# First attention of a four-layer kernel: the output projection of unit u-2 moves behind the sums of unit u, into the free bank of their pair and in four 32-column tiles; the row maxima are turned in 64x64 tiles

## What is computed

```python
# B=2, T=1024, D=128, 16 heads, head size 8 for q and k, 64 for v
cp   = leaky_relu(x @ Wc.T + bc)
q, k, v = cp[..., :128], cp[..., 128:256], cp[..., 256:]
attn = softmax(q @ k.T / sqrt(8))            # per head, 1024 x 1024
out  = attn @ v                              # 16 heads x 64 columns = 1024
s    = leaky_relu(out @ Wo.T + bo) + x
```

## Time and profile before

| | |
|---|---|
| time, median of 3 runs | 1037.55 us |
| the runs | 1035.93, 1037.55, 1039.93 us |
| profiled execution: span from the first to the last instruction | 1034.0 us |
| profiled execution: own time | not listed apart from the span; the median is 3.5 us above the span |
| TensorE busy (matmuls) | 926.5 us, 90% |
| VectorE, GpSimd, ScalarE busy | 773.7, 633.5, 547.7 us |
| mean granted TensorE clock | 0.955 |
| attention, sums of unit 0 to sums of unit 28 | 185.1 to 590.7 us |
| attention, its last three units and end | 590.7 to 653.5 us |

### The profile page before, as it was taken

The page is one execution under the profiler, slowest core; times in us unless marked ns, Lnnn a source line. Parts: engine busy times, 40 slices in busy tenths (PEclk is TensorE's granted clock), DMA queues, the critical chain, the costliest instruction groups (busy, mean ns, idle before and its releaser), DMA issues.

```text
span 1034.0 us, 20151 instructions
## 1 busy us (share of the span) xinstructions
PE 926.5 (90%) x7298; PEld 476.8 (46%) x7298; DVE 773.7 (75%) x1300; ACT 547.7 (53%) x927; POOL 633.5 (61%) x555
## 2 busy tenths in 40 slices
PE   5799997999999999999989997799966766799997
PEld 3346554233333333333323334788955322368785
DVE  5864777888888888887888726774599999995513
ACT  1474445666666666666657784342454032257363
POOL 5570415788778667886877882033567878862412
PEclk9899998999999999999999998899999797799999
DMA  9353424111020101011101123467830200234562
GB/s 318 136 182 116 137 79 130 45 48 47 17 57 28 57 23 49 30 54 54 39 21 45 39 74 112 159 203 211 276 106 10 72 22 19 96 94 144 146 192 67
DMA packets 92273, 96.99 MB, mean 94 GB/s; under 512 B 23184, under 2 KB 68624, under 8 KB 91920
## 3 DMA queue, kind: packets, MB, share of 16 engines
q1 hardware_dynamic: 87056, 85.21, 27.0%
q0 software_dynamic: 5120, 10.50, 3.4%
HBM read 70.43 MB, written 24.77 MB: 92 GB/s over the span
## 4 chain that ended last, share of the span: by engine, by line
PE 74%; DVE 12%; POOL 5%; issue 4%; DMA 2%; ACT 1%; SPq 0%; DVEq 0%; ACTq 0%; POOLq 0%
PE ps L255 71%; PE ps L258 3%; POOL ar L261 3%; DVE small L274 3%; DVE ar L261 2%; DVE ar L274 1%; POOL psum_sb L261 1%; DVE osb L274 1%; DVE acc_sb L261 1%; DMA psum_sb<-in_L_bv 1%; DVE ps L261 1%; DVE psum_sb L261 1%; POOL acc_sb L320 1%; POOL gT L320 0%; SPq L301 0%
## 5 line engine op out<-in xcount | busy, mean ns | idle before, releaser
L255 PE MATMUL ps<-ar 64*64 64x512 bf16 (+4 forms) x5312 | 541.1, 448 | 36.6 <-DVE ar L261 12.3
L255 PEld LDWEIGHTS ps<-ar 64*64 64x64 bf16 (+2 forms) x5312 | 268.5, 137 | 288.8 <-issue 102.3
L298 ACT ACTIVATE ar<-ps 128x1024 f32<-128x1024 f32 (+2 forms) x336 | 303.9, 908 | 156.7 <-PE ps L255 150.9
L274 DVE TENSOR_REDUCE small<-ps 128x2 f32<-128x1024 f32 (+2 forms) x276 | 307.1, 1139 | 46.3 <-PE ps L255 44.7
L261 POOL TENSOR_TENSOR psum_sb<-psum_sb,ar 128x1024 f32<-128x1024 f32 x91 | 214.8, 2360 | 48.8 <-DVE on_sb L261 38.6
L261 POOL TENSOR_TENSOR ar<-ar 128x512 f32<-128x512 f32 (+1 forms) x80 | 106.4, 1333 | 36.1 <-DVE ar L274 18.3
L320 POOL DMA_INDIRECT gT<-ysort,rt x48 | 46.0, 958 | 99.7 <-issue 98.5
L261 DVE TENSOR_TENSOR ar<-ps,ar 128x256 f32<-128x256 f32 (+4 forms) x56 | 56.5, 1012 | 52.0 <-PE ps L255 43.3
L261 POOL TENSOR_TENSOR psum_sb<-ar 128x1024 f32<-128x1024 f32 x32 | 75.8, 2368 | 27.9 <-ACT ar L298 25.1
L295 ACT COPY ar<-ps 128x256 f32<-128x256 f32 (+1 forms) x84 | 30.8, 383 | 88.1 <-PE ps L255 53.0
L255 PE MATMUL ps<-wA,xnT 128*128 128x512 f32 (+3 forms) x192 | 66.6, 461 | 4.7 <-DVE ar L261 1.6
(11 more groups left out here) (159 smaller groups left out, 1050.0 us busy)
## 6 DMA issues: line engine op xcount, KB each, us to landing
ar<-in_L_up SPq DMA_DIRECT2D x48, 384.0 KB, 4.0
ar<-in_L_b SPq DMA_DIRECT2D x32, 322.0 KB, 3.6
rec_sb<-lscr SPq DMA_DIRECT2D x64, 128.0 KB
scr<-ar SPq DMA_DIRECT2D x48, 128.0 KB, 2.0
ar<-xsort SPq DMA_DIRECT2D x40, 128.0 KB, 2.4
ysort<-ar SPq DMA_DIRECT2D x40, 128.0 KB, 3.8
ar<-scr SPq DMA_DIRECT2D x32, 112.0 KB
xsort<-xs SPq DMA_DIRECT2D x12, 256.0 KB, 6.8
```

Source lines behind the costliest of these rows:

```text
L255: return self.e.matmul(o, l, r, start=start, stop=stop) if self.e else Nothing()
L274: return self.e.tensor_reduce(o, a, AX.X, op, negate=True) if negate else self.e.tensor_reduce(o, a, AX.X, op)
L298: return self.e.activation(o, a, fn, **kw) if self.e else Nothing()
```

## The change

The projection of unit u leaves k = 12 for k = 17, that is from step 8u+20 to step 8u+25, the step of the sums of unit u+2; there it follows the sums directly, writes into the second bank of their pair instead of a pair of its own, and is cut into four matmuls of 32 output columns. VectorE's `acc_sb` piece goes from k = 12 to k = 18. Units 30 and 31 keep k = 12. The turned maxima (but for the first ones) become two 64x64 transposes into the two banks of a pair, with one copy over both. The waits name both banks of a pair. In `SIDE_B` all pieces behind about step 125 stand 6 steps later, and none later than 256.

```diff
+    def proj_step(u):
+
+        return 17 if u < 30 else 12
...
-            for b in banks:
+            for b in banks if len(banks) > 1 else (banks[0], banks[0] + 1):
                 pe.wait_ge(*vacant(b))
...
-            pe.tr(pb[0:48, 0:128], nsp[:, 48 * k:48 * k + 48], identb).then_inc(*filled(b, ("rowsT", B)))
+            pe.wait_ge(*vacant(b + 1))
+            for n in range(2):
+                r = slice(64 * n, 64 * n + 64)
+                ins = pe.tr(ps[:, b + n, :].bitcast(BF16)[0:48, 0:64], nsp[r, 48 * k:48 * k + 48], identb[r, r])
+            ins.then_inc(*filled(b, ("rowsT", B)))
...
             if k == 1:
                 b = take(ring[0])
                 pe.wait_ge(*vacant(b))
+                pe.wait_ge(*vacant(b + 1))
+                beside_sums[u] = b + 1
...
-            if k == 12:
+            if k == proj_step(u):
                 pi = 2 * (g % 4) + pr
-                b = take(ring[0])
+                b = beside_sums[u + 2] if u < 30 else take(ring[0])
                 pe.wait_ge(*vacant(b))
                 pe.wait_ge(*at("scaled", u))
...
-                pe.mm(ps[:, b, :], wA[:, 1280 + 128 * pi:1408 + 128 * pi],
-                      on_sb[:, 512 * (u % 2):512 * (u % 2) + 512]).then_inc(*filled(b, ("proj", u)))
+                for r in range(0, 128, 32):
+                    ins = pe.mm(ps[r:r + 32, b, :], wA[:, 1280 + 128 * pi + r:1312 + 128 * pi + r],
+                                on_sb[:, 512 * (u % 2):512 * (u % 2) + 512])
+                ins.then_inc(*filled(b, ("proj", u)))
...
+            unit_tail(x // 8 - 3, x % 8 + 16)
...
                 s, b0 = g % 3, take(ring[0])
                 pe.wait_ge(*vacant(b0))
+                pe.wait_ge(*vacant(b0 + 1))
...
-            if k == 12:
+            if k == (18 if u < 30 else 12):
                 pi = 2 * (g % 4) + pr
                 dst = acc_sb[:, c0:c0 + CW]
                 dve.wait_ge(*at("proj", u))
...
-        "207 route.2 211 route.2 213 route.2 route.2 route.2 ln.1.0 220 route.2 ln.1.0 221 route.2 222 route.2 223 "
+        "213 route.2 217 route.2 219 route.2 route.2 route.2 ln.1.0 226 route.2 ln.1.0 227 route.2 228 route.2 229 "
```

More of the change, by code:

```diff
@@ L681, in tensor_program @@
         ring = [(4, 5, 6, 7)]
+        beside_sums = {}
         def ln(layer, c):
@@ L748, in max_rows @@
             pe.wait_ge(*at("rows_split", B))
-            pe.tr(pb[0:48, 0:128], nsp[:, 48 * k:48 * k + 48], identb).then_inc(*filled(b, ("rowsT", B)))
+            if B == 0:
+                pe.tr(pb[0:48, 0:128], nsp[:, 0:48], identb).then_inc(*filled(b, ("rowsT", B)))
+                return
+            pe.wait_ge(*vacant(b + 1))
[3 more added lines that the diff above has]
+            ins.then_inc(*filled(b, ("rowsT", B)))
         def max0():
@@ L1803, in max_rows @@
                 act.wait_ge(*at("rows1_in", B - 2))
-            pb = ps[:, bank["rowsT", B], :].bitcast(BF16)
-            act.acp(mT[:, 128 * k:128 * k + 128], pb[0:48, 0:128]).then_inc(*emptied(("rowsT", B), ("rows", B)))
+            b, dst = bank["rowsT", B], mT[:, 128 * k:128 * k + 128]
+            if B == 0:
+                ins = act.acp(dst, ps[:, b, :].bitcast(BF16)[0:48, 0:128])
+            else:
+                ins = act.acp(v3(dst, 64), ps[0:48, b:b + 2, :].bitcast(BF16)[:, :, 0:64])
+            ins.then_inc(*emptied(("rowsT", B), ("rows", B)))
         def max0():
```

## The result

The changed kernel takes 1094.2 us (median of 4 runs, 1092.33 to 1095.38) against 1037.12 for the kernel before (4 runs): a ratio of 1.057 with a 95% interval of 1.0541 to 1.0598, slower by 57 us. The forecast was 1073 with a range to 1088; the direction was right, the size 21 us short. The span of the profiled execution is 1090.5 us, 56.5 more than before.

A forecast was written before the change was run, and what follows sets the result against it. TensorE was taken as the bound (98% busy). Waits less savings +33.4, two exceptions -0.9, turned maxima -2.7, first and last units -2.7, end +8.8 sum to +35.9 on 1034.0; with 3.5 for the median, 1073 us, range 1058 to 1088.

The forecast's parts named there:

- The wait: In 24 units TensorE's scores of step 3 wait for VectorE's `acc_sb` to free their bank: 1.84 us each.
- the two exceptions: Two units where side work takes the pair first: wait covered, only 0.45 us of savings left each, -0.9 together.
- The savings: On TensorE per unit: 0.29 us from the projection behind the sums, 0.16 from the scores of step 3 and their maxima.
- Turned maxima: In every second unit their extra 0.64 us goes, but a new wait of 0.43 comes: -2.7 us in all.
- The end: Behind the sums of unit 31: the late last scatter delays SyncE's row loads and all behind, +8.8 us, bounds 0 and 9.8.
- The side work that moves by six steps: Side pieces shifted in the table meet other moments of VectorE: costed at nothing, bound 4 us either way.
- one scatter stands between GpSimd's last additions: In the last units, with unit 29's reciprocal no longer behind an `acc_sb`: together -0.7 us.
- The clock rival: TensorE's clock falls in half of the 24 new waits, 1.65 us lost each: +20, 1093 us; chance 0.10.

The follow-up runs named there:

- e1_acc17: The changed kernel with VectorE adding the projection one step earlier (k = 17), ahead of the reduction: 1137.13 us, ratio 1.0215 to the kernel before.
- e4_tiles_only: The kernel before with only the projection cut into four 32-column matmuls at its old place (k = 12): ratio 0.9987.
- e9_one_scatter: The kernel before with one GpSimd scatter moved from behind step 246 to behind step 252: 1128.73 against 1119.42 us, ratio 1.0073.
- e2_side_only: The kernel before with only the new side table, shifted by six steps: 1135.49 against 1114.5 us, ratio 1.0182.
- e19_pool_late: The kernel before with only GpSimd's side entries from step 216 on moved six steps later: 1131.46 against 1114.41 us, ratio 1.0163.
- e16_after_early: The changed kernel, but in the side table only entries from 127 to 164 move by six: 1156.31 us against 1119.92 for the kernel before, ratio 1.0324.
- before_again: The kernel before, unchanged, traced again on one of the four chips of the experiments: sums of unit 0 to 31 in 444.2 us.
- e7_pool_free: The kernel before without GpSimd's wait for `scaled` at k = 2: 1160.13 against 1119.92 us, ratio 1.0346.

## Why the prediction was wrong

**The wait: right, and 0.09 too small.** Four rows gave 2.91 - 1.07 = 1.84, and by the same count the trace has 3.01 - 1.07, some 1.93; the difference is the last row, 0.83 where 0.74 was taken. In 24 units that is 2 us. 24 of 26 units have it, and the two exceptions are units 19 and 25. But they didn't give back 0.45: unit 19 takes 16.95 us instead of 13.88. TensorE waits there 1.06 us for VectorE's side piece `xs`, which stands ahead of the reduction, and 1.05 for GpSimd at its end.

**The savings: right.** Without the wait a unit is 13.29 (`e1_acc17`), 0.45 under before, just 0.29 + 0.16. The parts come out too. In `e1_acc17` the scores of step 3 start 4.03 us behind the sums, before 3.17: the projection takes 0.86 there, against 1.16 at its old place. And the maxima follow these scores after 0.22 instead of 0.39. `e4_tiles_only` shows that the 0.29 is not the tiles' alone (0.06) but needs the place behind the sums, as the prediction had it. The savings are there beside the wait too: 13.74 + 1.93 - 0.46 = 15.21.

**Turned maxima: right in sum, by some luck.** 0.43 taken, 15.66 - 15.21 = 0.45. The prediction had the transposes below 0.1 and hidden in a wait of 0.43; in the trace they take 0.19, and the maxima two groups behind start 0.2 later than elsewhere:

```profile
345.67 0.41 PE L255 MATMUL ps<-ar 64*64 64x512 bf16 x4
...
346.12 0.41 PE L255 MATMUL ps<-ar 64*64 64x512 bf16 x4
```

The reduction that has to free their pair ends at 346.07.

**The end: right.** +8.8 forecast, +10.2 in the profile, +8.2 in the times of `e9_one_scatter`.

**The step that failed** is "The side work that moves by six steps meets other moments of VectorE; I cost it at nothing, since it is the same work, with a bound of 4 either way". The table costs 20 us by itself (`e2_side_only`), 8 of them the end that I had counted, 12 not: three times the bound. There are two things in it. In the last units TensorE is shorter and GpSimd is the bound, so each scatter that comes late stands between additions for which the sums wait; `e19_pool_late` shows this, with 4.9 us in units 28 to 30 from GpSimd's entries alone. And "the same work" isn't the same time: VectorE's pieces that fall beside GpSimd's additions take up to six times their own (2.10 for 0.34), likely a good part of the 4.4 us in units 15 to 21; this is read from the traces and no run singles it out. The prediction had read GpSimd's rows there only for the last scatter, and even gave "one scatter stands between GpSimd's last additions; together -0.7": it was +2.6 in place of -1.6 in units 28 to 30.

**A second part of some 9 us** arises without the late entries: `e16_after_early` lost 36.4 us, where the terms without the end give 27.1. Some 2 of it are the 0.09 of each wait. Some 7 lie in units 15 to 21, where more of VectorE's work is held than in `e2_side_only` (6.4 us against 2.5): with the wait the side work meets GpSimd's additions more often. No run takes these meetings alone. The prediction costed the wait and the side work apart; their meeting is the other half of the same step. In the changed kernel `on_sb` of unit 20 is held too, and the wait behind it is 3.65 us (rows at the end).

**The clock rival: false, though its 1093 lies next to the measured 1094.** That is chance. Windows before and behind a wait of 1.76 us, the whole stretch from the sums of unit 0 up to the wait of 3.65, and the window behind that one (the clock is the third number from the end):

```profile
340.00:342.90 2.90, 1.14 (x20) 0.23 (x12) 2.42 (x3) 1.02 (x1) 0.72 (x1) 1.00 0.04 3
342.90:346.20 3.30, 3.26 (x42) 1.18 (x46) 2.45 (x2) 2.38 (x4) 3.16 (x2) 1.00 0.02 5
...
184.04:506.90 322.86, 279.74 (x3112) 88.70 (x3108) 256.39 (x306) 192.50 (x214) 228.07 (x165) 1.00 0.13 37
...
507.00:510.30 3.30, 3.30 (x28) 1.54 (x32) 1.39 (x2) 1.61 (x2) 3.16 (x2) 0.57 0.02 5
```

Behind 1.76 us the granted clock stays at 1.00, 2.4 GHz, and so it does over the first 17 of the waits for `acc_sb`, one of 2.39 among them; behind 3.65 it is 0.57, so most of that stretch is at 1.2 GHz, as behind the one in the earlier trace rows. It falls once more behind the wait of 4.04 in unit 25 (0.51 from 593.0 to 596.3). So in these units the clock cost one fall more than before, not twelve. The wait of the earlier trace rows, 2.63 us, comes again in `before_again` with TensorE at rest from 577.8 to 580.4, and there the clock stays at 1.00 behind it: the length alone doesn't decide. The swing of which the Trainium skill speaks ("TensorE: Matmul & The Clock Gate", "A second HAM failure mode: psum-queue depth-cycling") came at none of the regular waits.

## What to carry to other kernels

When a result moves into a bank that the next round takes, count what stands ahead of its reader in the reader's queue: here four rows of the trace, counted from start to start, gave the wait to within 0.1 us, and swapping two pieces changed it by exactly the length of one. A table of side work that is shifted as a whole is a change of its own: ask in each stretch which engine is the bound there, above all where TensorE's part gets shorter, count what the shift puts ahead of that engine's work, and look which operations with sources in SBUF will run beside each other. And a piece that is moved ahead of another on one engine can close a loop over three (`acc_sb`, `on_sb`, GpSimd, sums), which shows only where that loop is the bound.

## What the runs showed of the hardware

VectorE's `on_sb`, with both sources in SBUF, is held while GpSimd runs an addition on SBUF. In the changed kernel it happened by chance:

```profile
503.32 2.34 POOL L261 TENSOR_TENSOR psum_sb<-ar 128x1024 f32<-128x1024 f32 x1
503.64 2.57 DVE L261 TENSOR_TENSOR on_sb<-osb,rec_sb 128x512 f32<-128x512 f32 x1
506.13 0.68 DVE L261 TENSOR_TENSOR acc_sb<-acc_sb,ps 128x512 f32<-128x512 f32 x1
506.29 2.35 POOL L261 TENSOR_TENSOR psum_sb<-psum_sb,ar 128x1024 f32<-128x1024 f32 x1 [0.63 <-DVE on_sb L261]
...
506.95 1.44 PE L255 MATMUL ps<-ar 64*64 64x512 bf16 x12 [3.65 <-DVE acc_sb L261]
```

It ends 0.55 us after the addition, about its own 0.68; in `e7_pool_free` 20 such ones take 2.8 us, and the kernel loses 3.5%. GpSimd's wait for `scaled`, behind which stands no data, pays for itself. This is the rule of the Trainium skill ("SBUF — State Buffer", section "SBUF: two separate sides", the shared port pair as an exclusive lock: an operation of VectorE with two inputs in SBUF and one of GpSimd that reads SBUF don't run together, the later one waits for the whole of the other), and the trace agrees, with 2.81 us. `acc_sb`, which reads PSUM and SBUF, kept its 0.68 or 0.69 beside such additions (506.13, beside the one from 506.29).

A change of tile shape costs TensorE about 0.1 us: two groups of four 32-column fp32 matmuls take 0.86 ahead of their own shape, 0.97 ahead of 64x64 tiles.
